# The zero rows behind each expert's rows: 128 for each expert, sent from the final counts, in a routed mixture of experts kernel

## The chip, the cores and the metric

One core of a Trainium2 chip runs the kernel. The metric is the time on the device in microseconds (us), the median of several runs. TensorE is called PE in the profile, VectorE DVE, ScalarE ACT, GpSimd POOL and SyncE SP.

## The reference, cut to what matters

`x` is 2 x 1024 tokens of 256 values. A gated cross attention (16 heads, 154 context tokens) is added to it, and then a gated mixture of experts, with N = 2048 tokens, E = 8 experts and the two best experts of each token:

```python
h = layernorm(x)                                  # x: after the attention
xf = (layernorm(h) * gamma + beta).reshape(-1, D)
logits = clip(xf @ router_w.T, -CLAMP, CLAMP)
probs = clip(softmax(logits), ROUTER_EPS, 1.0)
topk_p, topk_i = top_k(probs, 2)
dense_gate = zeros((N, 8)).at[arange(N)[:, None], topk_i].add(topk_p)
for eid in range(8):
    xe = xf * dense_gate[:, eid:eid + 1]
    gate, up = split(xe @ gate_up_w[eid].T, 2, axis=-1)
    out = out + (silu(gate) * up) @ down_w[eid].T
return x + tanh(g_ffn) * (h + out)
```

An expert's work is done only for the tokens that chose it, so the 4096 rows (two for each token) are sorted by expert on the chip.

## The kernel before, in words

The program has two blocks of instructions for all engines, one behind the other.

**The attention block** walks over NI = 4 groups of four 128-token tiles. Attention of group i and the routing of group i - 1 are interleaved, and the routing of the last group (called NI in the code) stands alone behind the attention of the last group. For each group the router picks two experts for each token (`choose`, lines 995 to 1005, semaphore `chosen`), TensorE counts the rows of each expert (`rows_before`), DVE adds the counts up in `base_cnt` (`count_rows`, line 1013) and turns them into a row number in `expert_queue` (`number_rows`, line 1020, semaphore `row_sb`). `expert_queue` is a tensor in device memory with a region of REG = 2176 rows for each expert, and a row is 257 values of 4 bytes: 256 of the gated token and the token's number. POOL writes the rows with indirect DMAs of 128 rows each (`send_rows`, line 438, eight of them for a group, semaphore `rows_q`).

The buffer `rows`, from which they are sent, is used again by each group. For the last group ACT fills it (line 839): it waits for `chosen` and for the landing of all rows sent before (line 836), then raises `gated`. POOL waits for `gated` (line 480) and for the landing of the zero rows (`pads_q`, line 481), and only then sends the last 1024 rows (line 483).

**The zero rows.** The second block reads an expert's rows in tiles of 128, and the last tile of an expert is rarely full. What lies behind the expert's last row must be harmless: rows of zeros whose token number points at 128 spare rows of the output. In the kernel before, DVE works out where they start from the counts without the last group (lines 1128 and 1129, `pad`, semaphore `pads`). SP then sends (TPI + 1) * P = 640 rows for each of the 8 experts (lines 304 to 308), with one register load from `pad` (line 306) and one DMA (line 307) for each expert. The rows of the last group are later written over the first part of them, which is why POOL waits for `pads_q`.

**The order on SP around the change**: the eight sends of zeros, the last two output DMAs (`send_output(NI - 1)`, line 298), waits for all output DMAs (`out0_q`, 310) and the first zero rows (`zero_q`, 311), waits for `order` (313) and `pos_ps` (314), the loads of the first expert's weights (`load_weights(sp, 0)`, a register load at 148 and two DMAs at 151, 1 MB and 0.5 MB), a wait for all rows (`rows_q`, 317) and for `table` (318), and two loads of 128 rows (`load_rows`, a register load at 156 and a DMA at 160).

**The order on DVE around the change**: after `number_rows(NI)` the experts are ranked by their number of tiles (lines 1155 to 1167, semaphore `order`) and the table of which tile is read in which turn is made (1169 to 1189, semaphore `table`).

**The expert block** runs 39 tiles. For each: a load of 128 rows (line 160), transposes (1262), 12 matmuls for gate and up (1279), SiLU (1349), transposes (1289), 12 matmuls down (1299), a scaled copy (1362), and a scatter-add of 128 rows to the output by an indirect DMA of POOL (1234). Each scatter-add waits for the landing of the one before (line 1231).

Of the kernel before, what the change touches and what calls it, by code (L numbers as in the profile page):

```python
# [5 lines left out]
ALU = mybir.AluOpType  # L6
# [9 lines left out]
P = 128  # L16
# [31 lines left out]
def gated_xattn_moe(nc, x, ctxT, g_x, g_f, Wq, Wk, Wv, Wo, bo, gamma, beta, rwT, guT, dnT, out):  # L48
# [5 lines left out]
    E = rwT.shape[1]  # L54
# [9 lines left out]
    TPI, GPI = 4, 2  # L64
# [16 lines left out]
    DUMMY = E * REG  # L81
    RW = D + 1
# [6 lines left out]
    with ExitStack() as ctx:  # L89
# [10 lines left out]
        queue = nc.dram_tensor("expert_queue", [E * REG + P, RW], F32)  # L100

        s = {}
# [43 lines left out]
        def load_weights(sp, rank):  # L146

            e = sp.value_load(order[0:1, rank:rank + 1] if isinstance(rank, int) else order[0:1, bass.ds(rank, 1)], min_val=0, max_val=E - 1)
            for src, raw in ((guT, gu_raw), (dnT, dn_raw)):
                w = src[bass.ds(e, 1)].rearrange("a (c p) f -> p (a c) f", p=P)  # L150
                sp.dma_start(pick(raw, rank).rearrange("p (c f) -> p c f", f=src.shape[2]), w).then_inc(s["w_in"], 16)
# [26 lines left out]
        with ExitStack() as actx:  # L178
            def asb(name, shape, dt=F32):
                return actx.enter_context(nc.sbuf_tensor(name, shape, dt))  # L180
# [28 lines left out]
            region0 = asb("region0", [P, TPI, E])  # L209
# [4 lines left out]
            base_cnt = asb("base_cnt", [P, E])  # L214
# [24 lines left out]
            padf = asb("padf", [P, E]); pad = asb("pad", [P, E], U16); zrow = asb("zrow", [P, RW])  # L239
# [34 lines left out]
            def _(sp):  # L274
# [18 lines left out]
                def send_output(i):  # L293

                    sp.wait_ge(s["out0"], 2 * (i + 1))
                    for b in range(B):
                        dst = out[bass.ds((b * (SEQ // P) + 2 * i) * P, 2 * P), :].rearrange("(t p) d -> p t d", p=P)
                        sp.dma_start(dst, out0[:, 2 * b:2 * b + 2, :]).then_inc(s["out0_q"], 16)
# [2 lines left out]
                    send_output(i)  # L301


                sp.wait_ge(s["pads"], 1)
                for e in range(E):
                    first = sp.value_load(pad[0:1, e:e + 1], min_val=0, max_val=DUMMY - (TPI + 1) * P)
                    sp.dma_start(queue[bass.ds(first, (TPI + 1) * P), :].rearrange("(a p) d -> p a d", p=P),
                                 zrow[:, :].unsqueeze(1).to_broadcast([P, TPI + 1, RW])).then_inc(s["pads_q"], 16)
                send_output(NI - 1)
                sp.wait_ge(s["out0_q"], 32 * NI)  # L310
                sp.wait_ge(s["zero_q"], 32)
# [2 lines left out]
                sp.wait_ge(s["pos_ps"], NI)  # L314
                load_weights(sp, 0)

                sp.wait_ge(s["rows_q"], 16 * 2 * NT)
                sp.wait_ge(s["table"], 1)
                load_rows(sp, 0, 0, False)
# [3 lines left out]
            def _(pool):  # L323
# [154 lines left out]
                number_tokens(NI)  # L478
                nc.gpsimd.drain()
                pool.wait_ge(s["gated"], 1)  # L480
                pool.wait_ge(s["pads_q"], 16 * E)
                for k in range(2):
                    send_rows(NI, k)
                pool.wait_ge(s["rows_q"], 16 * 2 * NT)
# [360 lines left out]
            def _(dve):  # L845
                v = nc.vector

                def then(ins):

                    v.drain()  # L850
                    return ins
# [44 lines left out]
                def scale_out(i, u):  # L896

                    half = (u % UPT) // 2
                    U = UPI * i + u
                    dve.wait_ge(s["pv"], U + 1)  # L900
                    nc.vector.reciprocal(rsum[:, :], psum_row[:, (u // UPT) % 2, 8 * half:8 * half + 8])
                    nc.vector.drain()  # L902
                    nc.vector.tensor_tensor(o_sb[:, half * 512:(half + 1) * 512].rearrange("p (h d) -> p h d", h=8),
                                            O_BANK[half][:, :].rearrange("p (h d) -> p h d", h=8),
                                            rsum[:, :].unsqueeze(2).to_broadcast([P, 8, DH]), ALU.mult).then_inc(s["o_sb"][half], 1)
# [109 lines left out]
                def number_rows(i):  # L1015

                    then(v.tensor_tensor(pos[:, :, :], pos[:, :, :], region0[:, :, :], ALU.add))
                    then(v.tensor_tensor(posm[:, :, :, :], pick1[:, :, :, :], pos[:, :, :].unsqueeze(1).to_broadcast([P, 2, TPI, E]), ALU.mult))
                    then(v.tensor_reduce(rowf[:, :, :], posm[:, :, :, :], AX_X, ALU.add))
                    v.tensor_copy(row[:, :, :], rowf[:, :, :]).then_inc(s["row_sb"], 1)  # L1020
# [103 lines left out]
                for u in range(UPI):  # L1124
                    slot(NI - 1, u)

                dve.wait_ge(s["zero"], 1)
                then(v.tensor_tensor(padf[:, :], base_cnt[:, :], region0[:, 0, :], ALU.add))
                v.tensor_copy(pad[:, :], padf[:, :]).then_inc(s["pads"], 1)
                scale_out(NI, -1)  # L1130
                block_stats(NI, 2)
                for u in (0, 2):
# [19 lines left out]
                count_rows(NI)  # L1152
                number_rows(NI)

                then(v.tensor_scalar(cnt1[:, :], base_cnt[:, :], float(P - 1), None, ALU.add))
                then(v.tensor_copy(cnti[:, :], cnt1[:, :]))
                then(v.tensor_scalar(cnti[:, :], cnti[:, :], P.bit_length() - 1, None, ALU.logical_shift_right))
# [7 lines left out]
                then(v.tensor_tensor(at_rank[:, :, :], at_rank[:, :, :], expert_no[:, :].unsqueeze(1).to_broadcast(by_expert), ALU.mult))  # L1165
                then(v.tensor_reduce(order_f[:, :], at_rank[:, :, :], AX_X, ALU.add))
                v.tensor_copy(order[:, :], order_f[:, :]).then_inc(s["order"], 1)

                then(v.tensor_tensor(ahead_of[:, :, :], ahead_of[:, :, :], tiles[:, :].unsqueeze(1).to_broadcast(by_expert), ALU.mult))
                then(v.tensor_reduce(start[:, :], ahead_of[:, :, :], AX_X, ALU.add))  # L1170
# [292 lines left out]
```

## Time and profile before

| what | us |
|---|---|
| median of 3 runs | 596.3 |
| lowest and highest run | 595.17, 599.48 |
| span of the profiled execution, first to last instruction | 602.2 |
| attention and routing, to the first row load's issue | about 377 |
| experts | about 225 |

The page gives no other time for the profiled execution than its span; the span lies 5.9 us over the median of the runs. Engine times stand from the start of the span. A line such as `359.73 3.30 ACT L839 ... x8` means that eight instructions of line 839 began at 359.73 us and that the last ended 3.30 us later. "To landing" is the time from the issue of a DMA to its completion as its semaphore shows it. In the page, TensorE is busy 522.3 us of 602.2 (87%), DVE 340.4 (57%), ACT 282.2 (47%) and POOL 231.9 (39%).

### The profile page before, as it was taken

To read this page: it belongs to the slowest core of one execution; us is meant where nothing else is said; L and a number is where in the kernel's file an instruction comes from. 1 tells how busy PE (TensorE), PEld (TensorE's weight loads), DVE (VectorE), ACT (ScalarE), POOL (GpSimd) and SP (SyncE) were. 2 spreads that over 40 slices of the span, in tenths; PEclk is the share of its full clock that TensorE was granted. 3 is DMA by queue.
4 is the path that set the end of the run, shared out by engine and by line. 5 is a ranking of instruction groups with operands and counts; after the bars stand their busy time and mean duration, and the time that the engine had idled before them with its cause. 6 is when DMAs were issued, how large, how long until landed. Compare 5 with 4: busy or idle time off the path is not lost.

```text
span 602.2 us, 12363 instructions
## 1 busy us (share of the span) xinstructions
PE 522.3 (87%) x3712; PEld 476.4 (79%) x3713; DVE 340.4 (57%) x783; ACT 282.2 (47%) x866; POOL 231.9 (39%) x319
## 2 busy tenths in 40 slices
PE   8999999999999999998998420699988998999991
PEld 6789999998989889898998410588877877888881
DVE  5856666677586585765756764255444544533330
ACT  3446556555465555564553112355543544533330
POOL 5160000337008780077704625043433433443333
PEclk9999999999999999999999755799999999999995
DMA  8500000001000100001010995636446436333322
GB/s 246 181 2 1 0 2 2 20 1 35 3 0 26 44 20 15 0 10 63 2 36 1 224 229 178 206 84 151 109 90 156 117 76 157 53 51 53 55 36 26
DMA packets 32372, 41.54 MB, mean 69 GB/s; under 512 B 3088, under 2 KB 28432, under 8 KB 32336
## 3 DMA queue, kind: packets, MB, share of 16 engines
q1 hardware_dynamic: 25184, 31.75, 17.9%
q0 software_dynamic: 7152, 9.33, 9.9%
q8 instruction: 21, 0.34, 0.2%
q14 instruction: 15, 0.12, 0.1%
HBM read 24.12 MB, written 16.95 MB: 68 GB/s over the span
## 4 chain that ended last, share of the span: by engine, by line
PE 34%; issue 26%; DVE 11%; ACT 8%; DMA 6%; POOL 6%; POOLq 3%; DVEq 2%; SPq 2%; another core or an unknown queue 1%; ACTq 0%
PE bank L603 7%; PE bank L581 6%; ACT probs L773 5%; PE bank L527 4%; POOL tok L1225 4%; PE bank L543 4%; PE bank L1279 3%; PE bank L557 3%; DMA expert_queue<-zrow 3%; DVE nmax L892 2%; POOLq L1233 2%; DMA out_dram<-yq,to_row 2%; PE bank L706 2%; PE bank L501 2%; DVEq L902 1%
## 5 line engine op out<-in xcount | busy, mean ns | idle before, releaser
L773 ACT ACTIVATE probs<-bank,nmax 128x154 f32<-128x154 f32 x256 | 97.6, 388 | 123.6 <-DVE nmax L892 119.3
L581 PE MATMUL bank<-vdiag,pT 128*128 128x128 f32 (+2 forms) x640 | 80.0, 272 | 7.1 <-DVE oT_lo L916 6.9
L581 PEld LDWEIGHTS bank<-vdiag,pT 128*128 128x128 f32 (+1 forms) x640 | 77.5, 191 | 10.5 <-DVE oT_lo L916 10.3
L1234 POOL DMA_INDIRECT out_dram<-yq,to_row x39 | 61.8, 1585 | 33.7 <-issue 24.1
L1279 PE MATMUL bank<-gu_hi,xqT_hi 128*128 x156 | 68.7, 441 | 1.1 <-DVE xqT_lo L1396 1.1
L892 DVE TENSOR_REDUCE nmax<-bank 128x2 f32<-128x308 f32 x128 | 60.1, 471 | 7.7 <-PE bank L543 6.8
L1279 PE MATMUL bank<-gu_hi,xqT_lo 128*128 x156 | 61.9, 397 | 0.0
L1279 PE MATMUL bank<-gu_lo,xqT_hi 128*128 x156 | 61.7, 396 | 0.0
L1408 DVE TENSOR_TENSOR hidT_lo<-bank,hidT_hi 128x512 fp32r<-128x512 f32 x39 | 26.9, 690 | 53.1 <-ACT hidT_hi L1355 53.1
L1403 DVE TENSOR_TENSOR hid<-hid,bank 128x512 f32<-128x512 f32 x39 | 26.8, 688 | 52.6 <-PE bank L1279 52.6
L557 PE MATMUL bank<-ident,probs 128*128 128x128 f32 (+1 forms) x320 | 46.2, 273 | 5.6 <-ACT xfT L786 2.9
L773 ACT ACTIVATION_READ_ACCUMULATOR probs<-bank,nmax 128x1 f32 x256 | 50.9, 199 | 0.0
L1232 POOL TENSOR_TENSOR to_row<-tok,no_offset 128x1 uint32<-128x1 uint32 x39 | 12.4, 317 | 95.0 <-DMA out_dram<-yq,to_row 90.8
L543 PE MATMUL bank<-k_hi,q_hi 128*128 128x308 f32 x128 | 46.8, 366 | 1.6 <-issue 1.0
L368 POOL TENSOR_TENSOR x<-x,bo_b 128x256 f32<-128x256 f32 (+1 forms) x16 | 12.4, 797 | 91.3 <-DVE xn L871 91.2
L1299 PE MATMUL bank<-dn_hi,hidT_hi 128*128 x156 | 44.4, 284 | 2.2 <-DVE hidT_lo L1408 2.2
L1362 ACT ACTIVATE yq<-bank,tgf 128x256 f32<-128x256 f32 x39 | 18.5, 475 | 55.7 <-DMA out_dram<-yq,to_row 53.8
L1299 PE MATMUL bank<-dn_lo,hidT_hi 128*128 x156 | 44.4, 284 | 0.0
L1299 PE MATMUL bank<-dn_hi,hidT_lo 128*128 x156 | 44.4, 284 | 0.0
L557 PEld LDWEIGHTS bank<-ident,probs 128*128 128x128 f32 (+1 forms) x320 | 37.3, 138 | 7.9 <-ACT xfT L786 3.6
L1262 PE MATMUL bank<-ident,xq 128*128 128x128 f32 x78 | 16.0, 287 | 27.6 <-DMA xq<-expert_queue 27.4
L543 PE MATMUL bank<-k_hi,q_lo 128*128 128x308 f32 x128 | 38.9, 304 | 0.0
(183 smaller groups left out, 1432.4 us busy)
## 6 DMA issues: line engine op xcount, KB each, us to landing
gu_raw<-in_gate_up_wT_dram SPq DMA_DIRECT2D x8, 1024.0 KB, 5.0
expert_queue<-zrow SPq DMA_DIRECT2D x8, 642.5 KB
xq<-expert_queue SPq DMA_DIRECT2D x39, 128.5 KB, 2.5
dn_raw<-in_down_wT_dram SPq DMA_DIRECT2D x8, 512.0 KB, 6.0
x<-in_x_dram SPq DMA_DIRECT2D x4, 512.0 KB, 13.0
out_dram<-out SPq DMA_DIRECT2D x8, 256.0 KB, 2.2
wq_raw<-in_L_xattn_Wq_dram SPq DMA_DIRECT2D x1, 1024.0 KB, 11.5
wo_raw<-in_L_xattn_Wo_dram SPq DMA_DIRECT2D x1, 1024.0 KB, 10.6
```

The lines of the kernel that those rows point to most:

```text
L527: last = nc.tensor.matmul(at[:, m * GT:(m + 1) * GT], w[:, c, cols], v[:, c, :], start=(n == 0), stop=(n == 5))
L543: last = nc.tensor.matmul(S_BANK[hf][:, 0:2 * NKB], q[par][:, pair, tok:tok + P], k[:, pair, par, :], start=(n == 0), stop=(n == 2))
L557: last = nc.tensor.transpose(dst, probs[u % 4][:, b * P:b * P + rows], ident[:, :])
L581: last = nc.tensor.matmul(at[:, col0 + j0 * DH:col0 + j0 * DH + n], pT[u % 2][0:rows, b, :], v, start=(b == 0), stop=(b == NBLK - 1), skip ...
L603: last = nc.tensor.matmul(M_BANK[1][:, 0:D], o[:, c, :], w[:, c, :], start=(n == 0), stop=(n == most - 1))
L773: last = nc.scalar.activation(probs[u % 4][:, j * NKB:(j + 1) * NKB], S_BANK[hf][:, m * NKB:(m + 1) * NKB], ACT.Exp, bias=nmax[:, u % 4, j ...
L892: nc.vector.tensor_reduce(nmax[:, u % 4, 2 * hf:2 * hf + 2], S_BANK[hf][:, 0:2 * NKB].rearrange("p (m k) -> p m k", m=2), AX_X, ALU.max, n ...
L1234: nc.gpsimd.indirect_dma_start(out[:, :], bass.IndirectOffsetOnAxis(to_row[:, 0:1], 0), yq[p % 2][:, :], None, compute_op=ALU.add).then_in ...
L1279: last = nc.tensor.matmul(at[p % 2][:, :], rows[:, c, :], weights(w, rank, c * FF2 + half * FF, FF), start=(n == 0), stop=(n == 3 * KD - 1))
L1299: last = nc.tensor.matmul(Y_BANK[p % 2][:, 0:D], h[:, c, :], weights(w, rank, c * D, D), start=(n == 0), stop=(n == 3 * KF - 1))
L1403: nc.vector.tensor_tensor(hid[p % 2][:, :], hid[p % 2][:, :], U_BANK[p % 2][:, :], ALU.mult).then_inc(s["e_hid"], 1)
L1408: nc.vector.tensor_tensor(hidT_lo[:, :, :].rearrange("p c t -> p (c t)"), HT_BANK[:, :], hidT_hi[:, :, :].rearrange("p c t -> p (c t)").bi ...
```

## The change

DVE no longer works out `pad` from the counts without the last group. It does so from the final counts: `padf` right behind `number_rows(NI)`, and the cast to `pad` right behind `order`. SP no longer sends 640 zero rows for each expert ahead of the last output DMAs. It sends 128 rows for each expert, with the same register load and one DMA each, behind `load_weights(sp, 0)`, and waits for their landing (`pads_q`) ahead of its wait for `rows_q`. POOL no longer waits for `pads_q` ahead of its last eight sends.

```diff
--- before.py
+++ after.py
@@ -301,11 +301,6 @@
                     send_output(i)
 
 
-                sp.wait_ge(s["pads"], 1)
-                for e in range(E):
-                    first = sp.value_load(pad[0:1, e:e + 1], min_val=0, max_val=DUMMY - (TPI + 1) * P)
-                    sp.dma_start(queue[bass.ds(first, (TPI + 1) * P), :].rearrange("(a p) d -> p a d", p=P),
-                                 zrow[:, :].unsqueeze(1).to_broadcast([P, TPI + 1, RW])).then_inc(s["pads_q"], 16)
                 send_output(NI - 1)
                 sp.wait_ge(s["out0_q"], 32 * NI)
                 sp.wait_ge(s["zero_q"], 32)
@@ -314,6 +309,11 @@
                 sp.wait_ge(s["pos_ps"], NI)
                 load_weights(sp, 0)
 
+                sp.wait_ge(s["pads"], 1)
+                for e in range(E):
+                    first = sp.value_load(pad[0:1, e:e + 1], min_val=0, max_val=DUMMY - P)
+                    sp.dma_start(queue[bass.ds(first, P), :], zrow[:, :]).then_inc(s["pads_q"], 16)
+                sp.wait_ge(s["pads_q"], 16 * E)
                 sp.wait_ge(s["rows_q"], 16 * 2 * NT)
                 sp.wait_ge(s["table"], 1)
                 load_rows(sp, 0, 0, False)
@@ -478,7 +478,6 @@
                 number_tokens(NI)
                 nc.gpsimd.drain()
                 pool.wait_ge(s["gated"], 1)
-                pool.wait_ge(s["pads_q"], 16 * E)
                 for k in range(2):
                     send_rows(NI, k)
                 pool.wait_ge(s["rows_q"], 16 * 2 * NT)
@@ -1124,9 +1123,6 @@
                 for u in range(UPI):
                     slot(NI - 1, u)
 
-                dve.wait_ge(s["zero"], 1)
-                then(v.tensor_tensor(padf[:, :], base_cnt[:, :], region0[:, 0, :], ALU.add))
-                v.tensor_copy(pad[:, :], padf[:, :]).then_inc(s["pads"], 1)
                 scale_out(NI, -1)
                 block_stats(NI, 2)
                 for u in (0, 2):
@@ -1152,6 +1148,7 @@
                 count_rows(NI)
                 number_rows(NI)
 
+                v.tensor_tensor(padf[:, :], base_cnt[:, :], region0[:, 0, :], ALU.add)
                 then(v.tensor_scalar(cnt1[:, :], base_cnt[:, :], float(P - 1), None, ALU.add))
                 then(v.tensor_copy(cnti[:, :], cnt1[:, :]))
                 then(v.tensor_scalar(cnti[:, :], cnti[:, :], P.bit_length() - 1, None, ALU.logical_shift_right))
@@ -1165,6 +1162,7 @@
                 then(v.tensor_tensor(at_rank[:, :, :], at_rank[:, :, :], expert_no[:, :].unsqueeze(1).to_broadcast(by_expert), ALU.mult))
                 then(v.tensor_reduce(order_f[:, :], at_rank[:, :, :], AX_X, ALU.add))
                 v.tensor_copy(order[:, :], order_f[:, :]).then_inc(s["order"], 1)
+                v.tensor_copy(pad[:, :], padf[:, :]).then_inc(s["pads"], 1)
 
                 then(v.tensor_tensor(ahead_of[:, :, :], ahead_of[:, :, :], tiles[:, :].unsqueeze(1).to_broadcast(by_expert), ALU.mult))
                 then(v.tensor_reduce(start[:, :], ahead_of[:, :, :], AX_X, ALU.add))
```

## Rows read from the trace of the kernel before

**Rows 1.** Busy time, clock, DMA share and GB/s by stretch around the change.
```profile
...
core 0: us, PE busy (x) PEld busy (x) DVE busy (x) ACT busy (x) POOL busy (x), PEclk, DMA share, GB/s
345.00:361.00 16.00, 3.60 (x24) 2.92 (x24) 10.07 (x45) 1.50 (x5) 4.41 (x6) 0.50 1.05 231
361.00:373.00 12.00, 0.00 (x0) 0.00 (x0) 6.57 (x16) 4.02 (x8) 7.27 (x8) 0.50 0.59 203
373.00:376.00 3.00, 0.00 (x0) 0.00 (x0) 0.36 (x1) 0.00 (x0) 1.04 (x2) 0.50 0.25 89
...
```

**Rows 2.** Chain of waits, 330 to 420 us, in order of time: start, us, what.
```profile
...
345.31 16.09 DMA expert_queue<-zrow
...
363.07 0.24 POOLq L436
...
373.37 3.15 DMA expert_queue<-rows,row_at
376.53 0.26 SPq L156
...
```

**Rows 3.** ACT in order of time, 326 to 382 us.
```profile
...
359.73 3.30 ACT L839 ACTIVATE rows<-xf,gate 128x256 f32<-128x256 f32 x8 [8.30 <-DMA expert_queue<-rows,row_at]
369.92 1.99 ACT L169 CAST gu_hi<-gu_raw 128x1024 fp32r<-128x1024 f32 x2 [6.89 <-DMA dn_raw<-in_down_wT_dram]
...
```

**Rows 4.** POOL in order of time, 326 to 390 us.
```profile
...
348.98 0.96 POOL L438 DMA_INDIRECT expert_queue<-rows,row_at  x1 [0.30 <-issue]
...
```

**Rows 5.** DVE in order of time, 326 to 382 us.
```profile
...
331.04 0.17 DVE L1129 CAST pad<-padf 128x8 uint16<-128x8 f32 x1
331.47 0.20 DVE L901 RECIPROCAL rsum<-psum_row 128x8 f32<-128x8 f32 x1 [0.26 <-PE bank L581]
...
355.67 0.19 DVE L1005 TENSOR_TENSOR chosen<-pick 128x32 bf16<-128x32 f32 x1
...
357.60 0.17 DVE L1020 CAST row<-rowf 128x8 uint32<-128x8 f32 x1
357.68 0.17 DVE L1155 TENSOR_SCALAR cnt<-base_cnt 128x8 f32<-128x8 f32 x1
...
360.39 0.17 DVE L1167 CAST order<-order_f 128x8 uint16<-128x8 f32 x1
...
366.32 0.32 DVE L1189 CAST table<-row_j 128x39 uint16<-128x39 f32 x1
...
```

**Rows 6.** The SP queue's own waits, 325 to 384 us: total us, times, longest.
```profile
...
SPq L148 <- DMA out_dram<-out: 1.8, 1, 1.8
...
```

**Rows 7.** DMA issues of the SP queue in order of time, 300 to 440 us.
```profile
...
332.18 14.84 SPq L307 DMA_DIRECT2D expert_queue<-zrow  x8
...
363.19 0.41 SPq L151 DMA_DIRECT2D gu_raw<-in_gate_up_wT_dram  x1
363.79 0.40 SPq L151 DMA_DIRECT2D dn_raw<-in_down_wT_dram  x1
377.27 1.50 SPq L160 DMA_DIRECT2D xq<-expert_queue  x2
...
```

**Rows 8.** Line 306: the register loads between two sends of zeros.
```profile
...
L306 SPq TENSOR_LOAD <-pad x8: 271/793/969, 331.2 to 343.7; - x8
...
```

**Rows 9.** Line 156: the register loads of the row loads, weights in flight.
```profile
...
L156 SPq TENSOR_LOAD <-table x4: 262/262/266, 376.5 to 382.1; - x4
...
```

**Rows 10.** DMA issues by line: count, KB each, median us to landing.
```profile
...
expert_queue<-zrow SPq DMA_DIRECT2D x1, 128.5 KB, 2.3
...
```

**Rows 11.** Line 1234, the scatter-adds: durations, and who waited for them.
```profile
...
L1234 POOL DMA_INDIRECT out_dram<-yq,to_row x39: 1550/1556/2412, 394.1 to 597.9; - x39
...
  POOL to_row L1232: 90.8, 38
...
```

**Rows 12.** TensorE's clock by stretch as the experts begin.
```profile
...
382.00:384.00 2.00, 2.00 (x7) 1.41 (x6) 0.72 (x1) 0.77 (x1) 0.00 (x0) 0.50 1.01 416
...
386.00:390.00 4.00, 3.06 (x18) 2.60 (x18) 1.72 (x3) 1.56 (x3) 0.19 (x1) 1.00 0.54 126
...
```

## The prediction

> **What bounds the kernel now.** I read the page first, then the chain of waits around 360 us, then each engine in order of time there, the SP queue's own waits, and the DMA issues. The page says that TensorE is busy 87% of the span, but the change touches none of its work. It touches the passage from attention to experts, where TensorE has nothing to do: 0.00 us of work in 12 us [rows 1]. The question is therefore what lets the experts begin.
>
> They begin with the first load of 128 rows. The chain comes to it like this [rows 2]: the last send of zeros lands at 345.31 + 16.09 = 361.4 us, POOL wakes at 363.07, its last send of rows begins at 373.37 and lands 3.15 later, SP starts the register load at 376.53, and the row load itself is issued at 377.27 [rows 7].
>
> The reader should not stop at the link from the zeros to POOL. POOL waits for several semaphores. ACT's eight copies, which raise `gated`, run from 359.73 to 363.03 [rows 3], so they ended after the zeros had landed (361.4) and just before POOL woke. The wait for `pads_q` that the change takes from POOL was not the last one. ACT is the one that was late, and it had idled 8.30 us for the landing of the group of rows sent before [rows 3]. The last of those sends ended at 348.98 + 0.96 = 349.94 [rows 4], yet the landing came at 359.7, 9.8 us later. In that stretch the DMA engines show a share of 1.05 and move 231 GB/s [rows 1]; the eight sends of zeros, 642.5 KB each, were issued from 332.18 on [rows 7]. That traffic of 5.26 MB is what holds ACT.
>
> Behind the row load everything hangs together. There are 39 scatter-adds, POOL waited 90.8 us for their landings in 38 waits, and they run from 394.1 to 597.9 us [rows 11]: one at a time, (597.9 - 394.1) / 38 = 5.36 us each. An earlier first tile moves the whole row of them, and so the end, by the same amount.
>
> **The change part by part.**
>
> *1. The zeros leave the stretch from 332 to 361.* The last send of all landed 3.15 us after its begin [rows 2]. By that the rows sent before land at about 348.98 + 3.15 = 352.1. ACT then waits for `chosen` alone, which DVE finishes at 355.67 + 0.19 = 355.86 [rows 5]. ACT begins at 355.9 instead of 359.73: 3.8 us earlier. Its copies and POOL's sends follow at the same spacing, with `row` ready at 357.77 [rows 5] in good time. All rows have landed at 376.53 - 3.8 = 372.7. If nothing else were late, this would be the gain.
>
> *2. SP's output wait.* SP waits 1.8 us at line 148 for the last output DMA, past the `order` semaphore [rows 6]; that DMA too lies behind the zeros. Without them it lands near 350 and the wait goes. `order` is there at 360.39 + 0.17 = 360.56 [rows 5]. From the end of the wait (362.4) to the end of the second weight DMA's issue (363.79 + 0.40 = 364.2 [rows 7]) are 1.8 us, so the weights are issued by 360.7 + 1.8 = 362.5.
>
> *3. The new sends of zeros on SP.* Each is a register load, some register work and one DMA. From the register load of a row load at 376.53 [rows 2] to its DMA at 377.27 [rows 7] are 0.74 us, so the first send is issued at 362.5 + 0.7 = 363.2. The next spacing is disputed. Two row loads of the same 128 rows take 1.50 us from the first issue to the end of the second, of 0.36 us, so 1.14 us from one to the next [rows 7]. The eight sends of before were issued from 332.18 [rows 7] to 345.31 [rows 2]: 13.13 / 7 = 1.88 us each, with register loads of 793 ns in the median, the quickest 271 [rows 8], where those of the row loads take 262, right behind 1.5 MB of weights too [rows 9]. The slow ones followed sends of 640 rows, five times what is now sent. I take 1.14. The last send is issued at 363.2 + 7 x 1.14 = 371.2. A send of just this shape, alone, lands after 2.3 us [rows 10]: 373.5. With 1.88 it would be issued at 376.3 and land at 378.6. These are the ends for this term.
>
> *4. The DMA engines.* They now get weights, rows and zeros in one stretch. Weights and rows (2.6 MB) took 12 x 0.59 + 3 x 0.25 = 7.8 us of full share [rows 1]. The zeros are 8 x 128.5 KB = 1.05 MB, at the 231 GB/s at which zeros and rows went before [rows 1] 4.6 us. Together 12.4 us, from 361.4 on: 373.8 if the engines never idle. If all 3.7 MB went at 231 GB/s it would be 15.9 us and end at 377.3. With 373.5 from part 3 and 373.8 from here, and some gaps, I take 374.2 for the landing of the last zeros. The rows (372.7) are then no longer last, and the wait that was removed from POOL comes back on SP.
>
> *5. DVE.* The old pair of instructions goes, but reciprocal 331.47 waited for TensorE behind it (331.04 + 0.17 = 331.21 [rows 5]): nothing. The new `padf` stands between 357.60 and 357.68, where an instruction behind an undrained one costs 0.08 us; so do the cast and the rest. `order` comes 0.1 later, which is in the 360.7 above, and `table` 0.2 later than 366.32 + 0.32 = 366.64 [rows 5], hidden by 7 us of waiting on SP. If that cover were gone it would cost 0.2.
>
> *6. The first weights* are issued 1.8 us earlier. ACT began to split them at 369.92 [rows 3], far ahead of the first rows: hidden. The wait on SP for `pads_q` has queued behind it only the two row loads, and behind those the next weights, which move with them.
>
> *Sum.* The register load of the first row load goes from 376.53 to 374.2: 2.3 us less. On the profiled execution that is 602.2 - 2.3 = 599.9. The median of the runs stands 5.9 under that execution's span and nothing in the change bears on this, so 596.3 - 2.3 = 594.0 us. A measurement of this kernel can tell about 1% (6 us) from no change; this is 0.4%.
>
> *A rule weighed.* The wait of ACT for a landing 9.8 us behind its issue is in rows 3 and 4. The Trainium skill, DMA: Bandwidth & Descriptors, section "Queues, rings and completion order", says that a DMA's completion count is written only after all earlier writes of the same DMA engine, over all its queues. The trace agrees in size: rows sent by 349.94 counted as landed at 359.7, near the end of the zeros at 361.4. By that rule zeros can also hold back the count of the last rows, so that these are not through at 372.7 but with the zeros, and 594.0 would stand while the case of the rows alone would lose chance.
>
> **The rivals.**
>
> *A. Zeros hidden, rows last.* If the zeros land by 372.7, the whole 3.8 us of part 1 come through: 592.5 us. For it: a send spacing of 1.14 brings them within a microsecond of that. Against it: they can't be issued before `order` and the weights, and 371.2 + 2.3 is already 373.5.
>
> *B. SP's sends become the wait, slower than before.* If the register loads take 0.8 us as in rows 8, because descriptors of weights and zeros pile up, the last zeros land at 378.6, 2.1 us after 376.5: 598.4 us. It decides from a spacing of (376.5 - 2.3 - 363.2) / 7 = 1.57 us. For it: the measured 1.88 for this very line. Against it: five times fewer rows each, and 262 ns behind weights.
>
> *C. The move does not come through.* All 3.7 MB at the slow rate end at 377.3 (376.5 to 377.3: 0.8 more, 597.1 us), or TensorE's clock takes part of the gain: it is granted 0.50 (1.2 GHz) at 382 to 384 and 1.00 (2.4 GHz) from 386 on [rows 12], after tens of microseconds with little work. If the rise kept its place in time although TensorE begins 2.3 us earlier, that extra stretch would run at half speed and 1.2 of the 2.3 us would be lost (595.2 us). So 595 to 597.
>
> *D. The executions differ.* The three runs span 4.3 us, and the profiled one is above them all; a change of the scatter-adds' pace by 0.15 us would be 39 x 0.15 = 6 us either way. Nothing in the change bears on it.
>
> **How the numbers follow.** The forecast (593 to 595) has a chance of 0.5, A 0.13, B 0.14, C 0.15, D 0.08. The likeliest gives 594.0. The low end takes A with an equal share of luck in the runs (596.3 - 595.17 = 1.1) and 1.2 for the clock: 590.2. The high end is B with 0.6 for a landing slower than 2.3: 599.0. Faster by over 1% (under 590.3) needs D or more than all of A: 0.06. Slower by over 1% (over 602.3) needs B with landings like the 6.1 us of the weights (363.79 to 369.9), or D: 0.05. Within 1%: 0.89.
>
> **What would show it.** In the profile after: the DMA share low from 332 to 360; ACT's copies at about 355.9, released by `chosen`; POOL's sends at 360.3 instead of 364.1; no output wait on SP; eight sends of zeros from about 363.2, 1.14 apart, with register loads near 262 ns; SP's last wait before the row load on zeros and not on rows, near 374.2; from there the same 225 us. The forecast is wrong if the rows are last (A), if the spacing is over 1.5 us (B), if the row load is 2 us earlier but the end is not (C), or if the span from the row load to the end has another length (D).

## The result and the profile after

The changed kernel takes 603.24 us (median of 20 runs, 599.85 to 606.52), the kernel before 599.64 us (20 runs, 595.17 to 601.79). The ratio is 1.0072 with a 95% interval of 1.0052 to 1.0092: 0.7% slower, where 0.4% faster was forecast. A second measurement (run a_after below) gave 1.0094, 1.0059 to 1.0129. The forecast of 594.0 us started from 596.3, the median of the first 3 of these 20 runs of the kernel before, 3.3 us under the median of all 20.

Ahead of the passage everything went as forecast. ACT in order of time, profile of the changed kernel:

```profile
...
350.30 3.30 ACT L838 ACTIVATE rows<-xf,gate 128x256 f32<-128x256 f32 x8 [4.46 <-DVE chosen L1004]
...
```

It answers to [rows 3]: ACT now waits for `chosen` (ready at 350.26) and starts 0.04 us after it. The wait for a landing is gone. All times of this stage lie 5.6 us earlier than in the trace before, since that trace had two waits in the attention that no other trace has (run e_before below); so I measure from marks on DVE: the end of the cast of `order`, 355.05 here, 360.56 before.

The DMA issues on SP and the chain of waits, both of the changed kernel:

```profile
...
356.18 0.41 SPq L151 DMA_DIRECT2D gu_raw<-in_gate_up_wT_dram  x1
...
357.95 9.84 SPq L315 DMA_DIRECT2D expert_queue<-zrow  x8
375.92 1.50 SPq L160 DMA_DIRECT2D xq<-expert_queue  x2
...
```

```profile
...
367.45 7.72 DMA expert_queue<-zrow
375.19 0.26 SPq L156
...
375.92 2.10 DMA xq<-expert_queue
...
```

The first row load is issued at 375.92, 20.9 us after `order`; in [rows 7] it was 377.27, 16.7 us after it. The eight sends of zeros go out from 357.95 to 367.45, (367.45 - 357.95) / 7 = 1.36 us apart. The last is not landed after 2.3 us as [rows 10] had it, but after 7.72.

SP's own waits, DMA issues by line, and the stretches around the change (these answer to [rows 6], [rows 10] and [rows 1]):

```profile
...
SPq L318 <- DMA expert_queue<-rows,row_at: 6.3, 1, 6.3
...
SPq L156 <- DMA expert_queue<-zrow: 1.1, 1, 1.1
...
```

```profile
...
expert_queue<-zrow SPq DMA_DIRECT2D x8, 128.5 KB, 8.2
...
```

```profile
...
core 0: us, PE busy (x) PEld busy (x) DVE busy (x) ACT busy (x) POOL busy (x), PEclk, DMA share, GB/s
332.00:350.00 18.00, 6.16 (x26) 4.99 (x24) 11.82 (x39) 0.81 (x2) 8.61 (x13) 0.58 0.21 73
...
359.00:365.00 6.00, 0.00 (x0) 0.00 (x0) 1.44 (x7) 0.00 (x0) 4.75 (x5) 0.50 1.05 363
365.00:371.00 6.00, 0.00 (x0) 0.00 (x0) 2.36 (x2) 1.99 (x2) 0.00 (x0) 0.50 1.12 172
371.00:376.00 5.00, 0.00 (x0) 0.00 (x0) 0.00 (x0) 0.00 (x0) 0.00 (x0) 0.50 0.18 24
...
```

SP waited 6.3 us for the rows and 1.1 more for the zeros. The zeros are last, as forecast, but the rows too landed late: their last send began at 364.01 and SP saw them some 10 us later (375.19 - 1.1 = 374.1), where 3.15 had been enough before [rows 2]. The semaphores' own updates in the trace agree: the rows' count is full at 374.06, that of the zeros at 375.18. The windows show why. From 359 to 365, with mostly weights, the engines move 363 GB/s at a share of 1.05. From 365 to 371, with zeros and rows alone, they are just as busy (1.12) and move 172 GB/s. The DMA is not idle and not short of work; its packets take longer. In the DMA records of the trace, averaged over one microsecond, a packet of 1028 bytes of zeros takes 47 ns at 363 us and 198 ns at 367 us, a packet of four rows 166 and up to 490 ns. Not every packet is slow: the median of the zeros' packets is 47 to 103 ns in each microsecond from 364 to 371, and a few take over 1 us.

### The profile page after: what moved, and what is told of

The parts are those of the page before. It is cut to its first block, busy times and chain, and to the rows that moved or that the text cites. A ratio compares the mean times of both kernels' runs of the same rounds, so it can differ in the third digit from the quotient of the medians.

```text
span 600.0 us, 12362 instructions
## 1 busy us (share of the span) xinstructions
PE 518.0 (86%) x3712; PEld 474.9 (79%) x3713; DVE 341.3 (57%) x783; ACT 282.4 (47%) x866; POOL 230.0 (38%) x319
## 4 chain that ended last, share of the span: by engine, by line
PE 32%; issue 27%; DVE 10%; POOL 10%; ACT 6%; POOLq 5%; DMA 4%; DVEq 3%; SPq 2%; ACTq 0%
PE bank L1277 5%; PE bank L602 5%; PE bank L580 5%; PE bank L526 4%; POOL tok L1223 4%; PE bank L542 3%; ACT probs L772 3%; PE bank L556 2%; PE bank L1297 2%; POOL rows L427 2%; DMA out_dram<-yq,to_row 2%; POOL expert_queue L438 2%; POOLq L1231 2%; PE bank L705 2%; DVE nmax L891 2%
## 5 line engine op out<-in xcount | busy, mean ns | idle before, releaser
L1260 PEld LDWEIGHTS bank<-ident,xq 128*128 128x128 f32 x78 | 10.4, 144 | 38.7 <-DMA xq<-expert_queue 29.7
```

The lines of the kernel that those rows point to most:

```text
L1260: last = nc.tensor.transpose(XT_BANK[:, c * P:(c + 1) * P], xq[p % 2][:, c * P:(c + 1) * P], ident[:, :])
```

## The experiments

The passage is given as the time from the end of `order`'s cast on DVE to the issue of the first row load, and that from the end of `chosen` to the same issue. "Start" is when `order` is ready, "rest" what follows the issue. "This" and "before" are medians in us, before on the same chip.

```
run                  this    before  ratio (interval)         start  order->load  chosen->load  rest
before (first trace)                                          360.6   16.7         21.4         224.9
e_before             594.41  595.60  1.0004 (0.9969, 1.0039)  354.6   13.8         18.5         222.3
n_before             591.61  590.82  one run                  355.1   14.5         19.2         220.3
o_before             594.00  590.82  one run                  355.1   14.0         18.7         223.2
after                603.24  599.64  1.0072 (1.0052, 1.0092)  355.1   20.9         25.7         224.1
a_after              599.33  594.60  1.0094 (1.0059, 1.0129)  353.3   19.8         24.6         223.3
b_early              599.08  594.60  1.0075 (1.0050, 1.0099)  358.1   13.2         17.9         224.6
c_early_late         605.12  594.60  1.0161 (1.0124, 1.0199)  361.6   18.8         23.6         222.9
d_early_spare        605.82  594.60  1.0171 (1.0130, 1.0213)  359.1   18.8         23.6         226.0
f_spare1024          601.81  595.60  one run                  361.7   15.7         20.5         222.7
m_partial            600.93  590.82  one run                  360.0   16.9         21.7         222.2
g_pitch              597.89  595.60  1.0055 (1.0035, 1.0075)  357.4   15.5         20.3         223.0
i_rows_first         605.91  596.15  one run                  353.6   25.2         30.0         225.3
j_zeros_first        597.15  596.15  one run                  355.3   16.0         21.4         224.0
k_zeros_first_pitch  596.29  596.15  1.0011 (0.9975, 1.0046)  355.6   15.0         20.4         226.7
h_before_pitch       594.04  595.60  0.9973 (0.9945, 1.0002)  357.7   12.1         16.8         222.6
l_before_pitch5      593.05  596.15  0.9951 (0.9921, 0.9982)  352.7   12.1         16.8         224.4
```

The first trace of before apart, passages repeat within 0.7 us among the traces of before and within 1.1 us between the two of after; start and rest are each of one execution and vary by some microseconds, so I read single traces for the passage only. The expectations of a_after to d_early_spare take the passage to SP's register load, 0.7 to 0.8 us ahead of the issue: their 16.0 and 20.1 us are the 16.7 and 20.9 of the table.

**a_after**: the changed kernel again.

> The changed kernel again, as the anchor for the runs beside it. The passage is measured from the end of the cast of order on DVE to SP's register load of the first row load: 16.0 us in the trace of before, 20.1 us in that of after. If the loss lies in this passage, both come back within 0.5 us and the ratio to before is 1.005 to 1.009. If it was a difference between two executions, the passage or the ratio moves.

The passage is 19.8 us, 1.1 under the first trace where 0.5 was allowed, and the ratio 1.0094. The loss is real, and it lies in the passage.

**e_before, n_before, o_before**: the kernel before, three more traces.

> The kernel before, once more with a profile. In its first trace the span (602.2 us) lay over that of every timed run, and DVE waited 5.0 and 4.1 us once each in the attention (at about 200 and 290 us), which the traces of after do not show. If that was this one execution, order is now ready at 350 to 353 us and the passage from order to the issue of the first row load is again 16.7 us. If the waits belong to the kernel, order comes again at 358 to 361 us.

> The kernel before, a third trace, for the passage alone: 16.7 us from order to the first row load's issue in its first trace, 13.8 in its second. If the first trace was typical, 16 to 17 again; if the second, 13 to 14.5, and the waits of 5.0 and 4.1 us in the attention are absent.

> The kernel before, a fourth trace, with the same two expectations: 16 to 17 us or 13 to 14.5 us from order to the first row load's issue.

The three give 13.8, 14.5 and 14.0 us. The first trace, on which the prediction rests, is the longest of the four by over 2 us. The waits of the first trace of before, whole span:

```profile
...
DVE x L923 <- remote: 9.1, 2, 5.0
...
```

These two waits of the attention (5.0 and 4.1 us) are in no other trace of this study, and its passage was 2.6 us over the mean of the other three (14.1). Whether that is this one execution or the place of the first measurement is open: there both kernels ran 4 to 5 us longer (599.64 and 603.24 against 594.60 and 599.33), and the first trace of the changed kernel has a longer passage too. The pairs fit the times each by itself: 20.9 - 16.7 = 4.2 us beside a loss of 0.72% (4.3 us), and 19.8 - 13.8 = 6.0 us beside 0.94% (5.6 us). From e_before, SP's DMA issues and ACT in order of time:

```profile
...
325.31 13.18 SPq L307 DMA_DIRECT2D expert_queue<-zrow  x8
...
355.43 0.41 SPq L151 DMA_DIRECT2D gu_raw<-in_gate_up_wT_dram  x1
...
368.33 1.50 SPq L160 DMA_DIRECT2D xq<-expert_queue  x2
...
```

```profile
...
351.66 3.30 ACT L839 ACTIVATE rows<-xf,gate 128x256 f32<-128x256 f32 x8 [6.23 <-DMA expert_queue<-rows,row_at]
...
```

ACT waited for the landing of the earlier rows here too, but its copies start 1.8 us behind `chosen`, not 3.9, and SP issues the weights 0.9 us behind `order` (355.43 - 354.56) and not 2.6: the output wait of [rows 6] is not there. So in these traces there was less to gain than the first trace showed.

**b_early**: no zeros in the passage. They are sent in the attention of the last group instead, from the counts without the last two groups, 1152 for each expert.

```diff
-                with sp.Fori(0, NI - 1) as i:
+                with sp.Fori(0, NI - 2) as i:
                     send_output(i)
+                sp.wait_ge(s["early"], 1)
+                for e in range(E):
+                    first = sp.value_load(early_pad[0:1, e:e + 1], min_val=0, max_val=DUMMY - (2 * TPI + 1) * P)
+                    sp.dma_start(queue[bass.ds(first, (2 * TPI + 1) * P), :].rearrange("(a p) d -> p a d", p=P),
+                                 zrow[:, :].unsqueeze(1).to_broadcast([P, 2 * TPI + 1, RW])).then_inc(s["early_q"], 16)
+                send_output(NI - 2)
...
-                    sp.dma_start(queue[bass.ds(first, P), :], zrow[:, :]).then_inc(s["pads_q"], 16)
...
+                pool.wait_ge(s["early_q"], 16 * E)
                 send_rows(NI - 1, 0)
```

> No zeros in the passage at all: 1152 zero rows for each expert (9.5 MB) are sent from the counts without the last two groups, while the attention of the last group runs and the DMA engines are nearly idle. Theory 1 (zeros and rows disturb each other at the DMA engines or in memory): the passage falls from 20.1 to about 12.1 us (rows alone last), packets of rows take the 160 to 190 ns that they take alone, and the kernel is 3.9 us faster than before and 8 us faster than after. Theory 2 (the rows and weights are slow by themselves once they start earlier, the zeros matter little): the passage stays at 17 us or more. Theory 3 (SP's sends are the cost, 10 us of issuing): also about 12 us; the next two runs tell it from theory 1.

The passage is 13.2 us from `order` (17.9 from `chosen`), against 20.3 with the late zeros: theory 1 or 3, not 2. But the kernel is as slow as the changed one. The price is paid in the attention. Windows of b_early while the early zeros run, and POOL in order of time:

```profile
...
core 0: us, PE busy (x) PEld busy (x) DVE busy (x) ACT busy (x) POOL busy (x), PEclk, DMA share, GB/s
256.00:298.00 42.00, 38.40 (x306) 37.24 (x304) 26.57 (x63) 22.92 (x91) 30.10 (x36) 0.96 0.96 252
...
```

```profile
...
280.77 1.04 POOL L395 TENSOR_TENSOR xin<-x,mv_b 128x512 f32<-128x512 f32 x1 [7.17 <-issue]
...
```

POOL's `xin` waits 7.17 us, 1.09 us in a_after at the same place. DVE and TensorE then wait for it: one step of the attention, from one update of `x` by DVE to the next, takes 22.12 us (271.47 to 293.59) where a_after takes 17.64. The page puts POOL's wait down to "issue", but in its queue a drain stands in the gap (`nc.gpsimd.drain()`, which the kernel puts in front of an instruction that reads an earlier one's result). The same drain in b_early and in a_after (durations in ns, shortest, median, longest):

```profile
...
L393 POOLq DRAIN  x2: 792/4314/7837, 272.8 to 283.2; - x2
...
```

```profile
...
L391 POOLq DRAIN  x2: 791/1274/1757, 273.5 to 277.8; - x2
...
```

The drain that begins at 272.8 stands behind eight sends of rows by POOL and takes 7.84 us instead of 1.76. It takes 7.5 to 8.9 us in the four other runs with early zeros as well. What it waited for the trace does not tell. What is shown is that DMA traffic in a stretch where the DMA engines had little to do was not free.

**c_early_late, d_early_spare**: early zeros, and the eight late sends back, once over the same rows, once into a spare tensor of the same shape.

```diff
+                    sp.dma_start(spare[bass.ds(first, P), :], zrow[:, :]).then_inc(s["pads_q"], 16)
```

> As the run with early zeros, and the eight late sends of 128 zero rows kept where the change has them, over the same rows. Theories 1 and 3: the passage is that of after again, 20 us. If it were the missing early traffic or code placement, it would stay near 12.

> As the run before it, but the eight late sends go to a spare tensor of the same shape instead of the expert queue, so they never touch memory next to the rows that are being sent. Theory 1a (what counts is the traffic): passage 20 us, 1028-byte packets at 140 to 200 ns in the worst microseconds. Theory 1b (what counts is the place, zeros next to rows in flight): packets near 50 ns, the last zeros land 2.3 to 3 us after their issue instead of 7.7, passage about 14 to 15 us. Theory 3 (issuing on SP): also 20.

18.8 us in both, 5.6 more than without the late sends. So it is the late sends that cost, and it does not matter whether they go next to the rows in flight. Theory 1b fell; theories 1a and 3 (SP's time to issue) both expected this and are not yet told apart.

**f_spare1024, m_partial**: the same late sends to the spare tensor, once of 1024 bytes with rows 1024 bytes apart, once of 1028 bytes with rows 1088 bytes apart.

```diff
-        spare = nc.dram_tensor("spare", [E * REG, RW], F32)
+        spare = nc.dram_tensor("spare", [E * REG, D], F32)
...
-                    sp.dma_start(spare[bass.ds(first, P), :], zrow[:, :])
+                    sp.dma_start(spare[bass.ds(first, P), :], zrow[:, 0:D])
```

> As the run with early zeros and late sends to a spare tensor, but the spare rows are 1024 bytes, one behind the other, instead of 1028. Same number of packets and bytes to within 0.4%. Theory of traffic (any 1 MB more in this stretch costs it): rows packets again at 300 to 450 ns, order to first row load 18.8 us. Rival, alignment (rows of 1028 bytes, which begin and end inside a 64-byte line, disturb each other when two streams of them are written at once): late packets at 47 to 60 ns, rows at 160 to 200 ns, and order to first row load about 15 us.

> As the run with early zeros and late sends of 1028 bytes to a spare tensor, but the spare rows lie 1088 bytes apart, so each row starts on a 64-byte line and only its last line is written in part. If crossing into the neighbour's line is what costs (two writes to one line): late packets at 47 to 60 ns and order to first row load 15.7 us, as with rows of 1024 bytes. If any partly written line costs, it stays at 18.8 us with rows at 300 to 450 ns.

DMA issues by line in the passage, of d_early_spare, f_spare1024 and m_partial in turn (the last number is the median us to landing), and the busiest stretch of the second:

```profile
...
spare<-zrow SPq DMA_DIRECT2D x8, 128.5 KB, 8.0
...
```

```profile
...
spare<-zrow SPq DMA_DIRECT2D x8, 128.0 KB, 5.9
...
```

```profile
...
spare<-zrow SPq DMA_DIRECT2D x8, 128.5 KB, 6.7
...
```

```profile
...
370.00:375.00 5.00, 0.00 (x0) 0.00 (x0) 2.00 (x2) 1.99 (x2) 1.31 (x2) 0.50 1.05 341
...
```

Four bytes less in each row, with the rows on a pitch of 1024, take 3.1 us off the passage (18.8 to 15.7). Zeros and rows overlap as before, and SP issues as many sends, but the engines move 341 GB/s at a share of 1.05. This is the run that names the cause of the slow packets: the length and place of the rows in memory, not the traffic as such. It accounts for 3.1 of the 5.6 us; the other 2.5 us (15.7 against 13.2) stay with quick packets, as the price of eight late sends: the last one is issued 11.4 us behind `order` and lands 3.6 us later, where without late sends the rows have landed after 12.4. The rows on a pitch of 1088 bytes with 1028 of them written lie between (16.9), where the expectation had 15.7 or 18.8, so neither of its two readings came out. A split into what rows sharing a 64-byte line cost (18.8 to 16.9) and what a line written in part costs (16.9 to 15.7) rests on one trace each, and its steps are hardly above the 1.1 us by which two traces of one kernel differ: it is not shown.

**g_pitch**: the changed kernel with rows of 1088 bytes everywhere.

```diff
+    RP = D + 16
-        queue = nc.dram_tensor("expert_queue", [E * REG + P, RW], F32)
+        queue = nc.dram_tensor("expert_queue", [E * REG + P, RP], F32)
...
-            rows = asb("rows", [P, 2, TPI, RW])
+            rows = asb("rows", [P, 2, TPI, RP])
...
-            sp.dma_start(xq[p % 2][:, :], queue[bass.ds(r * P, P), :])
+            sp.dma_start(xq[p % 2][:, :], queue[bass.ds(r * P, P), 0:RW])
```

The extra bytes of `rows` and `zrow` are zeroed once by POOL, ahead of its first loop.

> The changed kernel with rows of 272 values (1088 bytes, 17 lines of 64 bytes) in the queue, in rows and in zrow, so that each row begins and ends on a line; 6% more bytes. Alignment: zeros and rows at their undisturbed packet times, order to first row load falls from about 20.3 to 16 us or less, and the kernel is 4 us faster than the changed one, about as fast as before. Traffic: no change or slower.

The busiest stretch with zeros and rows, and the landings of g_pitch:

```profile
...
366.00:371.00 5.00, 0.00 (x0) 0.00 (x0) 2.36 (x2) 1.99 (x2) 1.00 (x2) 0.50 1.01 345
...
```

```profile
...
expert_queue<-zrow SPq DMA_DIRECT2D x8, 136.0 KB, 4.9
...
```

345 GB/s where the changed kernel had 172, and a passage of 15.5 us instead of 20.3. The kernel's ratio falls from 1.0094 to 1.0055, about 2.3 us, where 4 had been expected; the passage gained 4.8. The two intervals overlap, so the gain is shown in the passage and in the rate, not in the kernel's time. It is still slower than before, since its zeros are issued last while before had none in the passage: the last send goes out at 369.83, 12.4 us behind `order`, and lands at 372.12. Those are 2.3 us, the landing that part 3 of the prediction had taken from [rows 10]; the median of the eight is 4.9.

**i_rows_first**: the changed kernel, zeros sent only when the rows have landed.

```diff
+                sp.wait_ge(s["rows_q"], 16 * 2 * NT)
                 sp.wait_ge(s["pads"], 1)
...
                 sp.wait_ge(s["pads_q"], 16 * E)
-                sp.wait_ge(s["rows_q"], 16 * 2 * NT)
```

> The changed kernel with SP's wait for the landing of the rows moved ahead of the late zeros, so that zeros and rows are never in flight together. If it is the overlap of the two streams that makes both slow: rows land as without zeros, 3.2 us after their last send's begin (17 us after chosen), zeros alone take 47 to 60 ns a packet and land 2.3 us after issue, spacing 1.14 to 1.36 us; the first row load comes at chosen + 17 + 0.7 + 8.0 to 9.5 + 2.3 + 0.7 = 29 to 30 us after chosen, 4 to 5 us later than with the overlap (24.6 to 25.7). If zeros of 1028 bytes are slow by themselves, landings stay at 7 to 8 us and it comes at 34 us or later.

```profile
...
367.54 8.47 SPq L316 DMA_DIRECT2D expert_queue<-zrow  x8
378.79 1.50 SPq L160 DMA_DIRECT2D xq<-expert_queue  x2
...
```

```profile
...
expert_queue<-zrow SPq DMA_DIRECT2D x8, 128.5 KB, 2.3
...
```

Alone, zeros behave as in [rows 10]: 2.3 us to landing, 47 ns a packet, (8.47 - 0.36) / 7 = 1.16 us apart. The rows, without zeros beside them, landed 4.3 us after their last send's begin, where 3.2 had been expected and 10.1 measured in the changed kernel. The first row load comes 30.0 us after `chosen`, as expected of the overlap theory. So 1028-byte rows are not slow when the engines have time between them.

**j_zeros_first, k_zeros_first_pitch**: the changed kernel, zeros in front of the first weights; the second also with rows of 1088 bytes.

```diff
+                sp.wait_ge(s["pads"], 1)
+                for e in range(E):
+                    ...
                 sp.wait_ge(s["order"], 1)
                 sp.wait_ge(s["pos_ps"], NI)
                 load_weights(sp, 0)
...
                 count_rows(NI)
+                v.drain()
+                then(v.tensor_tensor(padf[:, :], base_cnt[:, :], region0[:, 0, :], ALU.add))
+                v.tensor_copy(pad[:, :], padf[:, :]).then_inc(s["pads"], 1)
                 number_rows(NI)
```

> The changed kernel with the zeros sent as soon as the final counts are there (pad made right behind the last count, ahead of number_rows), in front of the first expert's weights instead of behind them. Zeros go out 5 us earlier, weights 6 us later. Overlap theory: zeros and rows still overlap, so packets stay slow (100 ns and more), but the zeros end earlier: first row load 21 to 23 us after chosen instead of 25. If SP's place in the order were all: 18 us. The weights land late, about 20 us after chosen, and ACT's split of them may then be last.

> Both cures on the changed kernel: zeros in front of the weights and rows of 1088 bytes. Alignment theory: no slow packets, rows last again, first row load 17 us after chosen as in the kernel before with rows of 1088 bytes (16.8); weights land 17 to 19 us after chosen, nearly hidden. Kernel within 0.3% of before.

SP's issues, landings, and the stretch in which zeros and rows overlap, of j_zeros_first:

```profile
...
352.46 8.74 SPq L311 DMA_DIRECT2D expert_queue<-zrow  x8
362.06 0.43 SPq L151 DMA_DIRECT2D gu_raw<-in_gate_up_wT_dram  x1
...
371.30 1.50 SPq L160 DMA_DIRECT2D xq<-expert_queue  x2
...
```

```profile
...
expert_queue<-zrow SPq DMA_DIRECT2D x8, 128.5 KB, 3.4
...
```

```profile
...
356.00:362.00 6.00, 0.00 (x0) 0.00 (x0) 4.18 (x13) 0.00 (x0) 4.74 (x5) 0.50 0.63 213
...
```

This corrects the overlap theory. Zeros of 1028 bytes and rows are in flight together for 6 us and take 47 to 54 and 172 to 204 ns a packet: not slow, where I had expected 100 ns and more. The share is 0.63. What differs from the changed kernel is that no 1.5 MB of weights stand in front, so that zeros leave as SP issues them and do not pile up. The traces fit a cause with two parts: rows of 1028 bytes, and engines kept full by a backlog. The second part rests on j and i, one trace each. In j, SP's last wait was for the rows, which landed about 7 us after their last send's begin (363.53), and the weights came in at about the same time. Its passage is 16.0 us, 21.4 us after `chosen`; that this lies in the expected 21 to 23 is luck, since the packets were not slow. The k run, with no bad rows, is at 15.0: 20.4 us after `chosen` and not 17, so this expectation missed. Packets were quick (47 and 168 to 206 ns), but the weights, moved behind the zeros to 362.5, now share the end of the passage with the rows. Its time is that of before (1.0011).

**h_before_pitch, l_before_pitch5**: the kernel before with rows of 1088 bytes, the same edits as g_pitch.

> The kernel before with the same rows of 1088 bytes. Alignment: the 5.3 MB of zeros go faster than 231 GB/s, ACT's copies start at chosen (3.8 us earlier) and the kernel is 2 to 4 us faster than before. Traffic: the same as before or slower.

> The kernel before with rows of 1088 bytes again, with more rounds, since its first interval (0.9945 to 1.0002) just reached no difference. If the 1.7 to 2 us that the passage is shorter than in the second trace of before are real: ratio 0.995 to 0.998 and an interval below 1.

A stretch with zeros under way, first of e_before, then of h_before_pitch, and ACT of l_before_pitch5:

```profile
...
338.00:344.00 6.00, 3.74 (x17) 3.25 (x17) 3.12 (x6) 0.00 (x0) 4.84 (x5) 0.50 1.11 273
...
```

```profile
...
334.00:344.00 10.00, 4.75 (x26) 4.05 (x26) 7.15 (x19) 0.58 (x1) 4.64 (x7) 0.67 1.05 355
...
```

```profile
...
348.02 3.30 ACT L842 ACTIVATE rows<-xf,gate 128x256 f32<-128x256 f32 x8 [4.45 <-DVE chosen L1008]
...
```

The zeros go at 355 GB/s instead of 273. They are through before `chosen`, ACT starts 0.04 us behind it, and the passage is 12.1 us in both traces, 2.0 under before's 14.1. The kernel is 0.5% faster than before (0.9951, 0.9921 to 0.9982, twelve runs) and the fastest of all; the first measurement (0.9973) agrees. It gets the gain that the change was after, without moving the zeros.

## Why the prediction was wrong, point by point

The step that failed is part 4, the term for the DMA engines with zeros, rows and weights in flight together. Part 3 was off by less, and the base by an amount that is in doubt.

- **Part 1, the zeros leave 332 to 361, ACT starts at `chosen`**: right in mechanism. It starts 0.04 us behind. The size was off: 3.9 us in the first trace, 1.5 to 2.4 us in the other three traces of before.
- **Part 2, SP's output wait of 1.8 us goes**: it went, but before has it in its first trace only: weights were issued 0.9 us behind `order` in the three others. Worth nothing.
- Together the base is in doubt: 16.7 us of passage where three other traces have 14.1. The forecast of 374.2 for the landing means 374.2 + 0.74 - 360.56 = 14.4 us of passage. Against 14.1 that is no gain at all, even had each step come true; against 16.7 it is the forecast 2.3. A single trace whose span lay above all timed runs should have made the range of the base part of the forecast; it entered only as rival D.
- **Part 3, SP's sends**: first send 2.9 us behind `order`, forecast 2.6 (363.2 - 360.56). Spacing 1.36, forecast 1.14, between the two bounds; 7 x 0.22 = 1.5 us. Alone it was 1.16 (i_rows_first), so 1.14 was right for an unloaded queue.
- **Part 4, the DMA engines**: the step that failed. The sum gave 3.0 us from the last issue to its landing (371.2 to 374.2); it took 7.7: 4.7 us too little. The rows, which part 1 had land 3.15 us after their last send's begin, took 10.1. The terms 0.3 + 1.5 + 4.7 = 6.5 are the difference of 20.9 and 14.4. I had added the time of weights and rows to that of zeros at 231 GB/s, as if each stream kept its own rate. Zeros and rows together, pressed by a backlog behind the weights, went at 172 GB/s. With rows of 1024 bytes for the zeros or 1088 bytes for all, 341 and 345 GB/s; with 1088 the last zeros landed 2.3 us after their issue and the passage was 15.5 us, 1.1 over the 14.4 of the forecast. So the sum was nearly right for rows without slow packets. The second bound of this part, all 3.7 MB at 231, was still too fast.
- **Rival A** (rows last, 3.8 us of gain): the rows were indeed the longer wait (6.3 us against 1.1), but because they were slow too, not because the zeros were hidden; the zeros still landed last, as the forecast had it. **Rival B** (SP's spacing decides from 1.57): the spacing stayed at 1.36, so its point was not reached; the sign came out as it said, by another mechanism. **Rival C** (all at the slow rate) came nearest: its place was right, its price of 0.8 us far too low: 4.2 us between the first two traces, 6.2 between the mean passages (20.3 and 14.1). The part about TensorE's clock did not decide: from the row load to the first scatter-add passed 16.7 to 17.0 us before and 17.0 to 18.1 after, so it may hold up to 1.3 us in the first pair and nothing in the second.
- **The rule that was weighed**: the Trainium skill, DMA: Bandwidth & Descriptors, section "Queues, rings and completion order", has completion counts wait for earlier writes of the same DMA engine, over all queues. The rows' 10 us to landing in the changed kernel, beside zeros landing in 8.2, agree with it. In the DMA records of that trace the last packet of rows ends at 370.93 and their count is full only at 374.06, 3.1 us later; in g_pitch the two are 0.6 us apart. But in i_rows_first, with no zeros in flight, they are 2.0 us apart, so the runs don't separate the rule from writes that are simply slow to complete. Another rule bears on the slow packets: the Trainium skill, DMA: Bandwidth & Descriptors, section "How a descriptor splits into AXI transactions", says that for a piece that does not start at a multiple of 256 bytes the bytes from the multiple below it are fetched too and go unused. Rows on a pitch of 1088 bytes mostly miss such multiples too, yet they went at 345 GB/s and those of 1028 at 172; the rule alone does not explain the factor of two.
- **5 and 6**, DVE and the weights: as forecast. `order` and the cast of `pad` lie 0.08 us apart, and ACT split the weights at 365.40, 13 us before it turned to the first rows.

The mean passages differ by 6.2 us, the measured times by 0.72% of 599.64 (4.3 us) and 0.94% of 594.60 (5.6 us). Pair by pair, as above, passage and time agree within 0.4 us.

## What to carry to other kernels

When a transfer is moved into a stretch where others run, its landing time alone is no term for the sum, and neither is a rate measured with other partners; ask what stands in front of it and at what rate the mixture goes. Rows of 1028 bytes cost nothing measurable here while the DMA engines had slack, and up to half the rate when they had none; padding them to 1088 gained 0.5%, and moving the zeros lost 0.7%. And where one trace is the whole base, compare its span with the timed runs first, or take a second one: SP's wait of 1.8 us that the forecast counted on was in none of the three other traces.

## What the runs showed of the hardware that was not expected

- Writes to device memory in rows of 1028 bytes, two streams of them at full share: 172 GB/s (after, 365 to 371 us). In rows of 1088 bytes: 345 GB/s (g_pitch, 366 to 371). Zeros of 1028 against 1088 bytes in the kernel before: 273 (e_before, 338 to 344) against 355 GB/s (h_before_pitch, 334 to 344). That lines of 64 bytes are the unit is an inference from 1024, 1028 and 1088; no other length was tried.
- The same two streams at a share of 0.63 show no slow packets (j_zeros_first, 213 GB/s).
- 9.5 MB of writes during the attention cost about 4.5 us of it (22.12 against 17.64 for one step) through one wait of 7.2 us on POOL, in which a drain of 7.8 us stands that takes 1.8 without them (b_early and a_after; the wait is 7.8 and 8.2 us in c_early_late and f_spare1024).
